# A decoder of two layers on one core: ScalarE copies a step's turned attention weights ahead of the exponentials of a later step

## The chip, the core and the metric

The kernel runs on one core of a Trainium2 chip. Five engines work side by side, each through its own list of instructions in order: TensorE (PE, the matrix products; its weight loads have rows of their own, PEld), VectorE (DVE), ScalarE (ACT), GpSimd (POOL) and SyncE (SP, which starts transfers). They wait for each other through semaphores. The metric is the time of the whole program on the device, in microseconds (us).

## The reference

Two layers, each of attention, cross attention to a short context of 77 rows, and a mixture of experts, on x of 2 x 512 x 128, all in float32. The change lies in the attention of the second layer. Cut to that:

```python
# H, DQ, DV = 16, 64, 64; x is (2, 512, 128)
q = jnp.einsum('bsd,hqd->bhsq', x, w_q)
k = jnp.einsum('bsd,hqd->bhsq', x, w_k)
v = jnp.einsum('bsd,hvd->bhsv', x, w_v)
scores = jnp.einsum('bhsq,bhtq->bhst', q, k)          # causal mask follows
weights = jax.nn.softmax(masked / 8.0, axis=-1)
out = jnp.einsum('bhst,bhtv->bhsv', weights, v)
return jnp.einsum('bsf,df->bsd', cat(out), w_o)
```

Behind it stands a cross attention that keeps the 32 largest of 77 scores for each row and head, and then the experts.

## The kernel before, in words

The order of every engine's work is written out by hand, one block of code for each engine; nothing is scheduled by a planner. The attention of the second layer is a loop of 48 **steps** U = 0 to 47 that every engine's block runs in its own form (`for U in range(NU)`). The 1024 tokens make four blocks of 256. A step takes two heads, and of a block either both tiles of 128 query rows (steps 0 to 7 and 24 to 31, 128 + 256 = 384 columns of weights for a head) or one tile (steps 8 to 23 and 32 to 47, 384 or 512 columns in turn). For one step the work passes from engine to engine:

- TensorE `scores` (L2199) writes the scores to one of two pairs of PSUM banks; it waits until the exponentials of the step two earlier have read that pair.
- VectorE `row_max` (L1131) takes each row's maximum.
- ScalarE `exps` (L1562, instruction L1569) writes the exponentials to SBUF and adds up each row. It is two instructions a head pair or four, each followed by a short one that reads the sum.
- VectorE `row_inv` (L1137) inverts the sums, GpSimd `divide` (L704) multiplies.
- TensorE `turn` (L2228) turns the weights, 128 x 128 at a time, into PSUM banks 4 and 5 and raises `pt_ps`.
- ScalarE `evac_pt` (L1582), called **the copy** below, waits for `pt_ps` and copies the turned weights from those banks to SBUF (`prT`), then raises `ptc_ready`.
- TensorE `values` (L2231) multiplies them with the values of the heads, one step later.

The engines are in different steps at the same time. In the loop's turn U TensorE does the scores of U + 2 and turns the weights of U, ScalarE does the exponentials of U + 2 and the copy of U, GpSimd divides U + 1. Bank 4 has a second user: `project_qk` (L2168) writes a later head pair's queries and keys there, so it waits for the copy of the step before, and the turn behind it waits until ScalarE has copied the queries and keys out (`evac_qk`, L1553).

Around this pair ScalarE's turn has other copies. Ahead of it come the outputs of a head pair (L1577), queries and keys (L1553), values (L1559) and, in some turns, a first half of cross-attention scores (L1609) or of turned cross-attention weights (`weights_T`, L1630). Behind it come, in some turns, the normalised rows (`apply_two`, L1596), a second half of scores (L1609), the other half of turned cross-attention weights (L1630), a copy of a context (L1624), and its exponentials (L1617). TensorE's work for the cross attention shares bank 7, one use after the other: each use waits until ScalarE has copied out the one before.

The two waits that matter here are:

```python
def exps(U):                                  # L1562
    act.wait_ge(nmax_ready, through(U))       # the maximum
    if U >= 3:
        act.wait_ge(pt_ps, U - 2)             # the buffer of step U - 3 has been turned
...
def evac_pt(U):                               # L1579
    act.wait_ge(pt_ps, U + 1)                 # the weights of step U have been turned
```

Of the kernel before, what the change touches and what calls it, by code (L numbers as in the profile page):

```python
# [55 lines left out]
def width(U):  # L56

    c, at, i = UNIT[U][1][-1]
    return at + (c + 1) * P


def piece_of(U):

    if 12 <= U < 28:
        return divmod(U - 12, 4)
    if 29 <= U < 47:
        return 4 + (U - 29) // 3, (U - 29) % 3
    return None, None
# [41 lines left out]
def decoder(nc, x_in, ctx_in, a0_wq, a0_bq, a0_wk, a0_bk, a0_wv, a0_bv, x0_wq, x0_bq, x0_wk, x0_bk, x0_wv,  # L110
# [5 lines left out]
    with ExitStack() as held:  # L116
# [8 lines left out]
        def tiles(bank, width=P):  # L125

            return ps[:, bank, 0:TB * width].rearrange("p (t n) -> p t n", n=width)
# [1289 lines left out]
        def _(act):  # L1417
            def norm_T(n):
                b = NORMS[n][1]
                act.wait_ge(xnT_ps, n + 1)  # L1420
                act.activation(xnT[:, b * S:(b + 1) * S], ps[:, NORM_BANK[n], :], ACT.Copy)\
                   .then_inc(xnT_ready, 1)
# [128 lines left out]
            def evac_qk(j, bank):  # L1551
                act.wait_ge(qk_ps, j + 1)
                act.activation(qk_place(j), ps[:, bank, :].rearrange("p (w n) -> p w n", w=2), ACT.Copy)\  # L1553
                   .then_inc(qk_ready, 1)

            def evac_v(j, bank):
                g, h = j % NP, j // NP % 2
                act.wait_ge(v_ps, j // 2 + 1)
                act.activation(v_all[:, 2 * h:2 * h + 2, g:g + 2, :].rearrange("p t g n -> p t (g n)"),  # L1559
                               ps[:, bank, :].rearrange("p (t n) -> p t n", t=2), ACT.Copy).then_inc(v_ready, 1)  # L1560

            def exps(U):  # L1562
                s = U % 2
                act.wait_ge(nmax_ready, through(U))
                if U >= 3:
                    act.wait_ge(pt_ps, U - 2)
                for c, at, i in UNIT[U][1]:
                    for h in range(2):
                        act.activation(pr[U % 3][:, h, at:at + (c + 1) * P], ps[:, 2 * s + h, at:at + (c + 1) * P],  # L1569
                                       ACT.Exp, bias=nmax[:, i % 8, h:h + 1], accum_out=rsum[:, i % 8, h:h + 1])\  # L1570
                           .then_inc(ex_ready, 1)

            def evac_cat(j):
                act.wait_ge(av_ps, j + 1)
                if j % NP == 0 and j:
                    act.wait_ge(wo_ps, j // NP)
                act.activation(catT[:, j % NP, :], ps[:, 6, 0:2 * P], ACT.Copy).then_inc(cat_ready, 1)  # L1577

            def evac_pt(U):  # L1579
                n = width(U)  # L1580
                act.wait_ge(pt_ps, U + 1)
                act.activation(prT[U % 3][:, :, 0:n], ps[:, 4:6, 0:n], ACT.Copy).then_inc(ptc_ready, 1)  # L1582

            def norm_two(k, done, ready, source):
                act.wait_ge(done, k + 1)
                act.activation(xnT[:, 2 * P * k:2 * P * (k + 1)], source, ACT.Copy).then_inc(ready, 1)

            def evac_qc(k, source):
                act.wait_ge(qc_ps, k + 1)
                act.activation(qc[:, 2 * P * (k % 2):2 * P * (k % 2 + 1)], source, ACT.Identity, bias=bias("x1_bq"))\  # L1590
                   .then_inc(qc_ready, 1)

            def apply_two(k, rstd_done, ready):
                act.wait_ge(rstd_done, k + 1)
                for t in (2 * k, 2 * k + 1):
                    act.activation(xn[:, t, :], x[:, t, :], ACT.Identity, bias=offset[:, t:t + 1], scale=rstd[:, t:t + 1])\  # L1596
                       .then_inc(ready, 1)

            def evac_cn(k, source):
                act.wait_ge(cnT_ps, k + 1)  # L1600
                act.activation(cnT[:, 0:2 * P], source, ACT.Copy).then_inc(cnT_ready, 1)


            def scores(n, t, bank):
                act.wait_ge(half_ps, 2 * n + t + 1)
                if n >= 2:
                    act.wait_ge(gone_ready, n - 1)
                    act.wait_ge(dif_ready, n - 1)
                act.activation(sc[n % 2][:, t, :, :].rearrange("p h n -> p (h n)"), ps[:, bank, 0:4 * NC], ACT.Copy)\  # L1609
                   .then_inc(half_ready, 1)  # L1610

            def weights_x(n):
                q = n % 2
                act.wait_ge(dif_ready, n + 1)
                if n >= 2:
                    act.wait_ge(pkT_ps, 2 * n - 2)
                act.activation(pk[q][:, :, :, :], dif[q][:, :, :, :], ACT.Exp, scale=SCALEX)\  # L1617
                   .then_inc(exc_ready, 1)

            def evac_cx(n, bank):  # L1620
                act.wait_ge(cx_ps, n + 1)
                if n >= 8:
                    act.wait_ge(cn_ready, 2 * (n // 4 - 1))
                act.activation(cx[:, n // 4 % 2, n % 4, :], ps[:, bank, 0:8 * (DX + 1)], ACT.Copy).then_inc(cx_ready, 1)  # L1624

            def weights_T(n, t, bank):
                act.wait_ge(pkT_ps, 2 * n + t + 1)
                if n >= 1:
                    act.wait_ge(cx_ps, n)
                act.activation(pkT[t][:, :, :], tiles(bank)[0:NC], ACT.Copy).then_inc(pkT_ready, 1)  # L1630

            def tokens_high(k):
                act.activation(xt_hi[:, k % 2, :], xnT[:, 2 * P * k:2 * P * (k + 1)], ACT.Copy).then_inc(xin_ready, 1)
# [11 lines left out]
            for U in range(NU):  # L1645
                n, r = piece_of(U)
                spare = ps[:, 7, 0:2 * P]
                for j in range(4 * NP - 1):
                    if U == FIRST[j + 1] + 1:
                        evac_cat(j)  # L1650
                for j in range(3, 4 * NP):
                    if U == FIRST[j] - 3:
                        evac_qk(j, 4)
                        if j in (NP + 2, 2 * NP + 2):
                            tokens_high(j // NP + 1)
                for j in range(2, 4 * NP, 2):
                    if U == FIRST[j] - 1:
                        evac_v(j, 6)
                for k in range(3):
                    if U == STAGE[k + 1] + 3:  # L1660
                        evac_qc(k, spare)
                if U == 12:
                    scores(0, 1, 7)
                if U == 13:
                    scores(1, 1, 7)
                if U == 28:
                    scores(4, 0, 7)
                if r == 0 and n + 1 in EARLY:
                    scores(n + 1, 0, 7)
                if r == 2 and n >= 1:  # L1670
                    weights_T(n - 1, 1, 7)
                if U + 2 < NU:
                    exps(U + 2)
                evac_pt(U)
                for k in range(3):
                    if U == STAGE[k + 1] + 2:
                        apply_two(k, qn_rstd, qn_ready)
                for k in range(2):
                    if U == OUT[k] + 2:
                        apply_two(k, gn_rstd, gn_ready)  # L1680
                if U == 4:
                    norm_T(7)
                if U == 11:
                    scores(0, 0, 7)
                if U == 12:
                    scores(1, 0, 7)
                if U == 28:
                    scores(4, 1, 7)
                if r == 0 and n + 1 in EARLY:
                    scores(n + 1, 1, 7)  # L1690
                if r == 1 and n >= 1:
                    weights_T(n - 1, 0, 7)
                if r == 2 and n >= 1:
                    evac_cx(n - 1, 7)
                if r == 2:
                    weights_x(n)
                for k in range(3):
                    if U == STAGE[k + 1] + 2:
                        norm_two(k, qnT_ps, qnT_ready, spare)
                for k in range(2):  # L1700
                    if U == OUT[k]:
                        evac_cn(k, spare)
                    if U == OUT[k] + 3:
                        norm_two(k, gnT_ps, gnT_ready, ps[:, 6, 0:2 * P])
# [960 lines left out]
```

## Time and profile before

| | us |
|---|---|
| median of 3 runs | 602.57 (597.96 to 604.44) |
| profiled execution, its own time | 589.41 |
| its span, first to last instruction | 587.6 |
| the loop of 48 steps, in the span | about 137 to 392 |

The profile is one execution. Its times are counted from the span's first instruction. A group of rows gives busy time, and the idle time of the engine just before those instructions with what ended it. The loop is 255 us of the 587.6.

### The profile page before, as it was taken

To read this page: it belongs to the slowest core of one execution; us is meant where nothing else is said; L and a number is where in the kernel's file an instruction comes from. 1 tells how busy PE (TensorE), PEld (TensorE's weight loads), DVE (VectorE), ACT (ScalarE), POOL (GpSimd) and SP (SyncE) were. 2 spreads that over 40 slices of the span, in tenths; PEclk is the share of its full clock that TensorE was granted. 3 is DMA by queue.
4 is the path that set the end of the run, shared out by engine and by line. 5 is a ranking of instruction groups with operands and counts; after the bars stand their busy time and mean duration, and the time that the engine had idled before them with its cause. 6 is when DMAs were issued, how large, how long until landed. Compare 5 with 4: busy or idle time off the path is not lost.

```text
span 587.6 us, 12150 instructions
## 1 busy us (share of the span) xinstructions
PE 520.9 (89%) x3954; PEld 413.7 (70%) x3954; DVE 384.4 (65%) x2192; ACT 309.2 (53%) x776; POOL 224.3 (38%) x235
## 2 busy tenths in 40 slices
PE   4888789988898999988999889978999899999997
PEld 2565348846666666767677567667777678999997
DVE  3567865433422598774598899877948979644643
ACT  2343225427875677675875667555775555322222
POOL 5015930013434364662554656552821443430000
PEclk9999999998999999999989999989899999999999
DMA  4600206504000000000000000003510000010000
GB/s 121 204 1 15 63 13 183 171 10 153 1 1 1 1 2 2 1 2 1 2 2 2 2 1 2 1 2 108 176 36 11 15 20 20 19 28 2 28 1 10
DMA packets 24088, 21.03 MB, mean 36 GB/s; under 512 B 2175, under 2 KB 18643, under 8 KB 24027
## 3 DMA queue, kind: packets, MB, share of 16 engines
q1 hardware_dynamic: 23515, 19.21, 10.8%
q0 software_dynamic: 512, 1.05, 0.6%
q8 instruction: 33, 0.54, 0.4%
q14 instruction: 28, 0.23, 0.1%
HBM read 17.22 MB, written 3.03 MB: 34 GB/s over the span
## 4 chain that ended last, share of the span: by engine, by line
PE 65%; DVE 17%; ACT 12%; issue 4%; POOL 1%; DMA 1%; DVEq 0%; ACTq 0%
PE ps L1835 53%; PE ps L2228 4%; DVE nmax L1131 2%; ACT w_mem L1569 2%; ACT prT L1582 2%; PE ps L2290 2%; DVE wk L1186 2%; PE ps L2423 2%; DVE sel_mem L1013 2%; DVE top L1176 2%; ACT f_mem L1534 1%; DVE bn L844 1%; DVE xn L857 1%; PE ps L2482 1%; ACT pr L1569 1%
## 5 line engine op out<-in xcount | busy, mean ns | idle before, releaser
L1131 DVE TENSOR_REDUCE nmax<-ps 128x2 f32<-128x256 f32 (+1 forms) x64 | 51.2, 821 | 66.9 <-PE ps L1835 64.6
L1186 DVE MATCH_REPLACE8 wk<-top,wk 128x77 f32<-128x77 f32 x384 | 80.5, 223 | 0.0
L704 POOL TENSOR_TENSOR w_mem<-w_mem,rinv 128x256 f32<-128x256 f32 (+3 forms) x44 | 53.0, 1216 | 50.8 <-DVE rinv L1137 50.3
L1302 DVE TENSOR_TENSOR sel_mem<-gr,ps 128x512 f32<-128x512 f32 x47 | 32.2, 685 | 50.0 <-ACT gr L1771 49.5
L1771 ACT ACTIVATE gr<-ps 128x512 f32<-128x512 f32 x47 | 28.0, 596 | 60.1 <-PE ps L1835 59.9
L1176 DVE MAX8 top<-wk 128x8 f32<-128x77 f32 x384 | 57.9, 223 | 0.2
L1835 PE MATMUL ps<-cat_mem 64*128 64x256 f32 (+7 forms) x276 | 54.9, 470 | 1.5 <-ACT cat_mem L1553 1.5
L1569 ACT ACTIVATE w_mem<-ps,nmax 128x128 f32<-128x128 f32 (+3 forms) x88 | 44.4, 519 | 12.2 <-DVE nmax L1131 12.2
L735 POOL TENSOR_SCALAR wk<-wk 128x616 f32<-128x616 f32 x16 | 28.0, 1752 | 53.7 <-DVEq L1190 53.4
L1835 PE MATMUL ps<-prT,cat_mem 128*64 128x128 f32 x640 | 43.7, 285 | 1.4 <-DVE x L1211 0.9
L1582 ACT ACTIVATE prT<-ps 128x768 f32<-128x768 f32 (+1 forms) x48 | 42.6, 887 | 0.1
L628 POOL TENSOR_TENSOR rstd<-var_eps,minus_half 128x4 f32<-128x4 f32 x8 | 8.2, 1025 | 88.5 <-DVE var_eps L850 88.4
L1835 PEld LDWEIGHTS ps<-prT,cat_mem 128*64 128x64 f32 x640 | 35.9, 141 | 7.3 <-issue 4.2
L704 POOL TENSOR_TENSOR pr<-pr,rinv 128x768 f32<-128x768 f32 (+3 forms) x20 | 26.6, 1338 | 28.4 <-DVE rinv L1137 28.0
L1553 ACT ACTIVATE cat_mem<-ps 128x512 f32<-128x512 f32 x32 | 19.1, 598 | 32.0 <-PE ps L1835 32.0
L1835 PE MATMUL ps<-fd,sel_mem 128*128 128x128 f32 x256 | 34.5, 278 | 1.5 <-DVE sel_mem L1302 1.5
L2228 PE MATMUL ps<-ident,w_mem 128*128 128x128 f32 x212 | 29.0, 275 | 6.7 <-issue 4.0
L1835 PE MATMUL ps<-later,ident 128*128 128x512 bf16 (+1 forms) x131 | 32.8, 374 | 2.3 <-ACT sc L1609 1.1
L1835 PE MATMUL ps<-x_hi,w_hi 128*128 128x256 f32 x128 | 34.6, 304 | 0.0
L1835 PEld LDWEIGHTS ps<-fd,sel_mem 128*128 128x128 f32 x256 | 31.2, 192 | 2.9 <-DVE sel_mem L1302 2.8
L1835 PE MATMUL ps<-x_hi,w_lo 128*128 128x256 f32 x128 | 31.9, 282 | 0.0
L1835 PEld LDWEIGHTS ps<-vh,sel_mem 77*128 77x128 f32 x256 | 29.9, 192 | 2.4 <-issue 1.2
(352 smaller groups left out, 1338.4 us busy)
## 6 DMA issues: line engine op xcount, KB each, us to landing
w_mem<-in_L_ffn_W_dram SPq DMA_DIRECT2D x12, 256.0 KB, 3.2
f_mem<-in_L_ffn_Wg_dram SPq DMA_DIRECT2D x8, 256.0 KB, 2.8
f_mem<-in_L_ffn_Wu_dram SPq DMA_DIRECT2D x8, 256.0 KB, 3.2
f_mem<-in_L_ffn_Wd_dram SPq DMA_DIRECT2D x8, 256.0 KB, 3.9
sel_mem<-slot_dram SPq DMA_DIRECT2D x7, 256.0 KB
sel_mem<-in_L_ffn_W_dram SPq DMA_DIRECT2D x4, 256.0 KB, 3.9
xs_dram<-zero SPq DMA_DIRECT2D x1, 960.0 KB, 6.0
ys_dram<-f_mem SPq DMA_DIRECT2D x15, 64.0 KB, 1.5
```

Source lines behind the costliest of these rows:

```text
L704: pool.tensor_tensor(pr[s][:, :, at:at + n], pr[s][:, :, at:at + n], rinv[:, i % 8, :].unsqueeze(2).to_broadcast([P, 2, n]), ALU.mult)\
L735: pool.tensor_scalar(wk[q][:, :, :, :], wk[q][:, :, :, :], NEG, None, ALU.is_le)\
L1131: dve.tensor_reduce(nmax[:, i % 8, :], ps[:, 2 * s:2 * s + 2, at:at + (c + 1) * P], X, ALU.max, negate=True).then_inc(nmax_ready, 1)
L1176: dve.max(top[q][:, t, h, 8 * r:8 * r + 8], src[:, t, h, :]).then_inc(top_step, 1)
L1186: dve.match_replace(wk[q][:, t, h, :], top[q][:, t, h, 8 * r:8 * r + 8], src[:, t, h, :], GONE).then_inc(top_step, 1)
L1302: dve.tensor_tensor(hg[s][:, :], gr[s][:, :], ps[:, 2 * s + 1, :], ALU.mult)\
L1553: act.activation(qk_place(j), ps[:, bank, :].rearrange("p (w n) -> p w n", w=2), ACT.Copy)\
L1569: act.activation(pr[U % 3][:, h, at:at + (c + 1) * P], ps[:, 2 * s + h, at:at + (c + 1) * P], ACT.Exp, bias=nmax[:, i % 8, h:h + 1], accum ...
L1582: act.activation(prT[U % 3][:, :, 0:n], ps[:, 4:6, 0:n], ACT.Copy).then_inc(ptc_ready, 1)
L1771: act.activation(gr[j % 2][:, :], ps[:, 2 * (j % 2), :], ACT.Relu).then_inc(gr_ready, 1)
L1835: return pe.matmul(dst, lhsT, rhs, start=start, stop=stop, skip_group_check=shared)
L2228: last = pe.transpose(tiles(4 + h)[:, k, :], pr[U % 3][:, h, k * P:(k + 1) * P], ident[:, :])
```

## The change

Two calls in ScalarE's loop trade places: the copy of step U now stands ahead of the exponentials of step U + 2. Nothing else in the file differs, and the instruction lists of TensorE, VectorE, GpSimd and SyncE are the same as before.

```diff
                 if r == 2 and n >= 1:
                     weights_T(n - 1, 1, 7)
+                evac_pt(U)
                 if U + 2 < NU:
                     exps(U + 2)
-                evac_pt(U)
                 for k in range(3):
                     if U == STAGE[k + 1] + 2:
                         apply_two(k, qn_rstd, qn_ready)
```

ScalarE in turns 10 and 11, before. L1569 are the exponentials, L1582 the copy, L1596 the normalised rows, which wait for GpSimd.

```order
L1569 ACTIVATE w12_mem,rsum<-ps,nmax 128x384 [waits pt_ps,nmax_ready]
L1569 ACTIVATE w12_mem,rsum<-ps,nmax 128x384
L1582 ACTIVATE prT1<-ps 128x2x384 [waits pt_ps]
L1596 ACTIVATE xn<-x,offset,rstd 128x128 [waits qn_rstd]
L1596 ACTIVATE xn<-x,offset,rstd 128x128
L1586 ACTIVATE xnT<-ps 128x256 [waits qnT_ps]
L1577 ACTIVATE sel_mem<-ps 128x256 [waits wo_ps,av_ps]
```

The same place in the changed kernel:

```order
L1582 ACTIVATE prT1<-ps 128x2x384 [waits pt_ps]
L1569 ACTIVATE w12_mem,rsum<-ps,nmax 128x384 [waits pt_ps,nmax_ready]
L1569 ACTIVATE w12_mem,rsum<-ps,nmax 128x384
L1596 ACTIVATE xn<-x,offset,rstd 128x128 [waits qn_rstd]
L1596 ACTIVATE xn<-x,offset,rstd 128x128
L1586 ACTIVATE xnT<-ps 128x256 [waits qnT_ps]
L1577 ACTIVATE sel_mem<-ps 128x256 [waits wo_ps,av_ps]
```

The normalised rows now stand directly behind the exponentials, and the copy ahead of both.

ScalarE in turn 17, before. L1553 copies queries and keys, L1630 copies turned cross-attention weights, the first for this turn and the second for the next.

```order
L1553 ACTIVATE cat_mem<-ps 128x2x256 [waits qk_ps]
L1569 ACTIVATE w12_mem,rsum<-ps,nmax 128x512 [waits pt_ps,nmax_ready]
L1569 ACTIVATE w12_mem,rsum<-ps,nmax 128x512
L1582 ACTIVATE prT2<-ps 128x1024 [waits pt_ps]
L1630 ACTIVATE sel_mem<-ps 77x512 [waits pkT_ps] x2
```

The same place in the changed kernel:

```order
L1553 ACTIVATE cat_mem<-ps 128x2x256 [waits qk_ps]
L1582 ACTIVATE prT2<-ps 128x1024 [waits pt_ps]
L1569 ACTIVATE w12_mem,rsum<-ps,nmax 128x512 [waits pt_ps,nmax_ready]
L1569 ACTIVATE w12_mem,rsum<-ps,nmax 128x512
L1630 ACTIVATE sel_mem<-ps 77x512 [waits pkT_ps] x2
```

The wait for the turned weights (`pt_ps`) now holds back the exponentials and everything behind them.

## Rows read from the trace of the kernel before

**Rows 1.** The page: span; busy time, share and count by engine.

```profile
span 587.6 us, 12150 instructions
PE 520.9 (89%) x3954; PEld 413.7 (70%) x3954; DVE 384.4 (65%) x2192; ACT 309.2 (53%) x776; POOL 224.3 (38%) x235
```

**Rows 2.** Stretches: us, busy by engine (count), granted TensorE clock, DMA share, GB/s.

```profile
137.00:392.00 255.00, 228.91 (x1940) 170.54 (x1939) 180.32 (x1137) 173.31 (x462) 129.82 (x109) 0.99 0.01 4
...
299.50:302.90 3.40, 3.40 (x31) 2.66 (x28) 3.40 (x31) 2.72 (x8) 0.31 (x1) 1.00 0.00 0
302.90:306.30 3.40, 3.40 (x20) 2.48 (x19) 3.17 (x21) 1.70 (x7) 2.25 (x2) 0.50 0.02 5
```

**Rows 3.** Waits of TensorE, 137 to 392: us in total, times, longest us.

```profile
PE ps L1835 <- ACT prT L1582: 2.2, 4, 1.0
PE ps L2264 <- ACT xn L1596: 2.1, 1, 2.1
PE ps L2228 <- ACT prT L1582: 1.9, 5, 0.5
PE ps L1835 <- ACT sel_mem L1630: 1.9, 2, 1.2
PE ps L1835 <- ACT sc L1609: 1.7, 2, 1.1
...
PE ps L2264 <- ACT sel_mem L1624: 0.6, 2, 0.3
```

**Rows 4.** ScalarE by line, 137 to 392: count | busy us, mean ns | idle before.

```profile
L1582 ACT ACTIVATE prT<-ps 128x768 f32<-128x768 f32 x32 | 26.1, 817 | 0.1
...
L1630 ACT ACTIVATE sel_mem<-ps 77x512 f32<-77x512 f32 x18 | 10.6, 590 | 6.7 <-PE ps L2290 6.6
```

**Rows 5.** Timeline, step 23: start us, us, engine, line, operation, [idle before <-releaser].

```profile
252.01 1.06 PE L2228 MATMUL ps<-ident,pr 128*128 128x128 f32 x8
252.11 0.59 ACT L1559 ACTIVATE cat_mem<-ps 128x512 f32<-128x512 f32 x1
...
254.17 1.05 ACT L1582 ACTIVATE prT<-ps 128x1024 f32<-128x1024 f32 x1
...
255.27 0.39 PE L1835 MATMUL ps<-xt_hi,wT_lo 128*128 128x256 f32 x1 [1.02 <-ACT prT L1582]
```

**Rows 6.** Timeline, step 10.

```profile
186.05 0.83 PE L2228 MATMUL ps<-ident,w_mem 128*128 128x128 f32 x6
...
187.82 0.58 ACT L1569 ACTIVATE w_mem<-ps,nmax 128x384 f32<-128x384 f32 x1 [4.85 <-DVE nmax L1131]
...
188.95 0.81 ACT L1582 ACTIVATE prT<-ps 128x768 f32<-128x768 f32 x1
189.64 0.87 ACT L1596 ACTIVATE xn<-x,offset,rstd 128x128 f32<-128x128 f32 x2
```

**Rows 7.** Timeline, step 17.

```profile
220.77 0.60 ACT L1553 ACTIVATE cat_mem<-ps 128x512 f32<-128x512 f32 x1 [1.34 <-PE ps L1835]
...
221.47 1.06 PE L2228 MATMUL ps<-ident,pr 128*128 128x128 f32 x8 [0.73 <-issue]
...
222.61 1.02 ACT L1582 ACTIVATE prT<-ps 128x1024 f32<-128x1024 f32 x1
...
223.51 0.59 ACT L1630 ACTIVATE sel_mem<-ps 77x512 f32<-77x512 f32 x1
...
224.15 0.66 PE L2290 MATMUL ps<-ident,ex_mem 128*77 128x128 f32 x4
```

**Rows 8.** Timeline, step 45.

```profile
381.13 1.04 PE L2228 MATMUL ps<-ident,w_mem 128*128 128x128 f32 x8
...
382.59 0.69 ACT L1569 ACTIVATE pr<-ps,nmax 128x512 f32<-128x512 f32 x1 [1.88 <-DVE nmax L1131]
...
385.48 0.66 PE L2290 MATMUL ps<-ident,ex_mem 128*77 128x128 f32 x4 [2.42 <-ACT sel_mem L1630]
```

**Rows 9.** Timeline, step 39.

```profile
351.35 0.41 PE L2290 MATMUL ps<-ident,ex_mem 128*77 128x128 f32 x2 [0.23 <-POOL ex_mem L742]
```

## The prediction, made before the changed kernel ran

> **What bounds the kernel now.** I read the page first: TensorE is busy 89% of the span and no other engine over 65% [rows 1]. The table of stretches says the same of the loop: TensorE works 228.91 of its 255 us, ScalarE 173.31 [rows 2]. So TensorE sets the pace and the change can pay only out of its 26.1 idle us; ScalarE, which the change reorders, has 81.7 us to spare. The list of waits tells whose products TensorE stands still for. The copy ends 2.2 us of idle in four waits and 1.9 in five; normalised rows end 2.1, turned cross-attention weights (L1630) 1.9 in two waits [rows 3] and 2.42 in another [rows 8], halves of scores 1.7 [rows 3]. In these rows the copy is late because exponentials stand ahead of it on ScalarE, and the others because they stand behind both. The timelines of single turns then show which of the two orders would have served TensorE better.
>
> **What the change does on ScalarE.** Nothing is added or removed: the 48 copies, 0.81 to 1.05 us each [rows 5, 6], and the exponentials stay, and the other engines' lists don't change; no transfer moves. In 46 turns (in the last two there are no exponentials left) the pair trades places. With the copy first it starts when ScalarE is free and the turned weights are there; the exponentials start behind it, or when their maximum is there if that is later. Work behind the pair starts when the pair ends. That gives three kinds of turn.
>
> (a) *The copy itself is waited for.* Step 23: the eight transposes end at 252.01 + 1.06 = 253.07, ScalarE is free at 252.70, yet the copy starts at 254.17, behind exponentials, and TensorE stands still 1.02 us until it ends [rows 5]. With the copy first it runs from 253.1 to 254.2, and TensorE's product can start when the one before it ends, 1.0 us sooner. The next link, the copy of the queries and keys, then finds ScalarE in exponentials: they took from 252.6 to 254.2, so 1.5 us behind the copy's new end, to about 255.6. So 0.3 of the 1.0 is given back. There are nine such waits, 2.2 + 1.9 = 4.1 us [rows 3]. I take off 0.2 for the first, in step 1, where the turn behind it is paced by the queries and keys anyway; 0.3 for step 23; and 0.8 for two of 0.4 around 329 and 348 us, since in that stretch TensorE ends up waiting for GpSimd's product at 351.35 [rows 9], whose chain has neither copy nor exponentials in it. Left: 2.8 us.
>
> (b) *The maximum is late, and something behind the pair is waited for.* Step 10: the transposes end at 186.88, but ScalarE stands idle 4.85 us for the maximum until 187.82, and only then come exponentials, the copy at 188.95 and the normalised rows at 189.64 [rows 6], for which TensorE waits 2.1 us [rows 3]. With the copy first it lies inside that idle time (186.9 to 187.75), and the rows start at 188.9: 0.75 us saved, about one copy. The same holds where ScalarE idles 1.88 us for the maximum in step 45, with TensorE's longest wait of 2.42 us at its end [rows 8]: the transposes end at 381.13 + 1.04 = 382.17, ScalarE gets its maximum at 382.59, so 0.4 of the copy falls into idle time and is saved. A third turn like it is step 44, with a wait of 1.06 us for scores: 0.55. Sum 1.7 us.
>
> (c) *ScalarE is free before the weights are turned.* Step 17: ScalarE is free at 220.77 + 0.60 = 221.37 and today spends the next 1.24 us on exponentials, while TensorE turns the weights until 222.53; the copy starts at 222.61 without loss [rows 7]. With the copy first ScalarE waits out this 1.24 us and does the exponentials later, and the copy gains nothing. What is queued behind it is the turned cross-attention weights at 223.51, and TensorE takes them up at 224.15, at once [rows 7]: they come 1.24 us later, and so does TensorE. Transposes that end after ScalarE is free stand in some 30 of the 46 turns, most of them by 0.3 to 1.2 us, but in most the next item behind the pair is one that ScalarE would idle for, or its taker has time. The ones that bite, worked out in the same way: step 17 with 1.2, step 21 with 0.45, step 25 (0.35 on the existing wait of 1.2 us for L1630 [rows 3]), step 26 (0.3 on one of 0.3 for L1624 [rows 3]). In stage one (steps 0 to 7), losses and gains of 0.15 to 0.25 for the copies of head outputs cancel. Sum 2.3 us.
>
> The later exponentials themselves cost nothing by this reckoning. They move back by at most step 17's wait and copy, 1.24 + 1.02 = 2.3 us [rows 7]. VectorE inverts their sums only behind the next maximum, one turn on, GpSimd's product is taken up another turn later, and the scores that need their bank come two turns on. Going through the turns one by one I find none where the 2.3 us or less reach TensorE that way; if the margin were gone, VectorE would stand waiting for the sums, and GpSimd's product and the transposes would be late next.
>
> **The sum.** 2.8 + 1.7 - 2.3 = 2.2 us off the profiled execution's 589.41, to 587.2. The median of the runs, 602.57, stands 2.2% above that execution; the same share of it gives 600.3 us.
>
> **A bound for the clock.** The granted clock was 2.4 GHz nearly throughout and fell to 1.2 GHz (0.50) for 302.90 to 306.30, where 20 products were done [rows 2]; at the loop's mean of 1940 in 255 us it would have been 25.9, so one such stretch costs 5.9 products, 0.8 us, and at most half of its 3.4 us. TensorE was busy through the 3.4 us before it fell [rows 2], so I can't say that the change adds or removes such a stretch, and keep 0.8 either way for the range.
>
> **The rivals.**
>
> *Only gains.* The losses (c) are local arithmetic. If ScalarE's spare 81.7 us swallow them, 4.5 us are won: 598.0. For it: nearly every wait in (c) is followed by idle time of ScalarE. Against it: in step 17 the taker starts 0.05 us after its weights are copied, so nothing is there to swallow it. Chance 0.22.
>
> *Nothing.* What TensorE wins at the copy it loses at its next wait for ScalarE, as at step 23 with a third of it; the clock, or VectorE and GpSimd in the last third of the loop, take the rest. 602.6. Chance 0.21.
>
> *Slower: the wait for the turned weights holds up ScalarE's queue.* This is (c) at every place where turned cross-attention weights stand directly behind the pair. ScalarE has 18 copies of them, two for each of nine pieces [rows 4], and one of each two stands there; if all nine slip by step 17's 1.24 us and are taken up at once, 11.2 us are lost against 4.5 won: 6.7 us slower, 609.4. It decides where the transposes end more than about 1 us after ScalarE is free and TensorE's next use of bank 7 follows within that. For it: steps 17 and 21 are so. Against it: in the others I found the transposes done sooner or the taker later. Chance 0.12.
>
> The Trainium skill speaks for this rival: "TensorE: Matmul & The Clock Gate", section "Architectural detail: the array is 16× 32×32, not 1× 128×128", says that ScalarE's queue is a strict FIFO, so that nothing can pass a copy that waits. By that rule taken alone, with no slack anywhere, the time would be the rival's 609.4. The trace agrees on the order: in step 10 the copy, ready at 186.88, stood behind exponentials until 188.95 [rows 6]; what it doesn't decide is whether anyone waits for what is held up.
>
> **How the numbers follow.** The forecast has 0.45. The likeliest time is 600.3. The range must take in 598.0 and 602.6 and the clock's 0.8 on either side, scaled, and the spread of the runs shown (597.96 to 604.44, so 4.6 below and 1.9 above the median): about half of that spread below the first gives 595.5, and it all above the second with the clock gives 606. The slow rival lies outside. A difference under 1%, here 596.5 to 608.6, can't be told from none in this kernel. Faster than that needs the only-gains case with luck, 0.14; slower needs the slow rival, 0.09; the rest is 0.77.
>
> **What would show it.** In the profile after, the row of TensorE's waits for the copy should fall from 4.1 us to about 1; step 10's wait for normalised rows from 2.1 to about 1.3; the copy of step 10 should lie inside the wait for the maximum. ScalarE should show new idle time ended by TensorE in front of the copy (L1582), near zero now [rows 4], of 10 us or more, and TensorE a new wait of over 1 us for L1630 in step 17. TensorE's idle time in the loop should fall from 26.1 to about 24. I am wrong if the new waits for L1630 or for the queries and keys exceed what the copy's waits give back, or if VectorE's maxima come later because scores do.

## The result: about 3 us gained at equal clock, hidden under a spread of 14

Timed beside the kernel before on the same chips, the changed kernel took 590.17 us (median of 19 runs, 586.72 to 597.2) against 595.7 (19 runs, 590.8 to 604.44): a ratio of 0.9932, interval 0.9903 to 0.996. (Ratios, here and below, leave out runs over 1.5% above the fastest of their kernel; medians do not.) Timed again on another chip the ratio was 0.9996, interval 0.9952 to 1.004. The forecast had the sign and a change of under 1%, but the measured 590.17 lies outside 595.5 to 606, and even the kernel before was not where the forecast had put it: 595.7 and not 602.57. The granted clocks of the 19 runs before are not on record, so this pair alone can't tell how much of the 5.5 us between the medians is the order.

**The profile after.** The page's span and busy times, which answer to [rows 1]:

```profile
span 588.2 us, 12150 instructions
PE 522.5 (89%) x3954; PEld 416.3 (71%) x3954; DVE 384.5 (65%) x2192; ACT 311.6 (53%) x776; POOL 224.5 (38%) x235
```

The span is 0.6 us longer than before, 590.0 us as a run. The table of stretches says why (columns as in [rows 2]: us, busy by engine, granted clock); the first row is the loop, the other two a stretch at half clock and the one ahead of it:

```profile
137.40:392.40 255.00, 230.07 (x1941) 173.22 (x1939) 181.16 (x1142) 175.41 (x462) 130.29 (x110) 0.98 0.01 4
272.68:276.09 3.41, 2.71 (x25) 2.30 (x25) 1.12 (x11) 3.41 (x14) 0.00 (x0) 1.00 0.00 0
276.09:279.50 3.41, 3.41 (x17) 2.85 (x14) 2.44 (x15) 0.70 (x2) 1.27 (x2) 0.50 0.00 0
```

TensorE's idle time in the loop fell from 26.1 to 24.9 us, but its busy time rose by 1.2 for the same work: the granted clock was at half for 3.41 us three times (from 276.09, 320.47 and 385.32), before only once [rows 2].

TensorE's waits in the loop (us in total, times, longest), against [rows 3]:

```profile
PE ps L2290 <- ACT sel_mem L1630: 4.6, 4, 2.0
PE ps L1835 <- ACT sel_mem L1630: 2.3, 2, 1.6
PE ps L2264 <- ACT xn L1596: 1.4, 1, 1.4
PE ps L1835 <- ACT sc L1609: 1.2, 2, 0.7
PE ps L2264 <- ACT sel_mem L1624: 1.0, 2, 0.7
```

Both rows of waits for the copy, 4.1 us, are gone; the waits for normalised rows and scores shrank, those for L1630 and L1624 grew. ScalarE's side, by line (count | busy us, mean ns | idle before), against [rows 4]:

```profile
L1582 ACT ACTIVATE prT<-ps 128x768 f32<-128x768 f32 x32 | 26.1, 814 | 10.6 <-PE ps L2228 10.0
L1582 ACT ACTIVATE prT<-ps 128x1024 f32<-128x1024 f32 x16 | 16.4, 1024 | 11.2 <-PE ps L2228 11.2
```

ScalarE now idles 21.2 us in front of the copy, for the transposes: the "10 us or more" of the prediction.

The turns themselves. The timeline (start us, us, engine, line, operation, [idle before <-releaser]) of step 23, as [rows 5]:

```profile
251.05 1.06 PE L2228 MATMUL ps<-ident,pr 128*128 128x128 f32 x8
...
252.15 1.02 ACT L1582 ACTIVATE prT<-ps 128x1024 f32<-128x1024 f32 x1 [0.41 <-PE ps L2228]
...
253.23 0.39 PE L1835 MATMUL ps<-xt_hi,wT_lo 128*128 128x256 f32 x1
...
254.65 0.62 ACT L1553 ACTIVATE cat_mem<-ps 128x512 f32<-128x512 f32 x1
255.37 0.85 PE L2228 MATMUL ps<-ident,w_mem 128*128 128x128 f32 x6 [1.17 <-issue]
```

TensorE no longer waits 1.02 us for the copy, and as predicted finds the copy of the queries and keys (L1553) late: its wait there is 1.17 us, from 0.73 before. Step 10, as [rows 6]:

```profile
185.46 0.83 PE L2228 MATMUL ps<-ident,w_mem 128*128 128x128 f32 x6
186.32 0.81 ACT L1582 ACTIVATE prT<-ps 128x768 f32<-128x768 f32 x1 [2.94 <-PE ps L2228]
187.23 0.58 ACT L1569 ACTIVATE w_mem<-ps,nmax 128x384 f32<-128x384 f32 x1
...
188.36 0.87 ACT L1596 ACTIVATE xn<-x,offset,rstd 128x128 f32<-128x128 f32 x2
189.37 0.41 PE L2264 MATMUL ps<-ident,xn 128*128 128x128 f32 x2 [1.41 <-ACT xn L1596]
```

The copy lies inside the wait for the maximum and the rows come 1.41 us after TensorE is free, not 2.1. Step 17, as [rows 7]:

```profile
219.32 1.06 PE L2228 MATMUL ps<-ident,pr 128*128 128x128 f32 x8 [0.73 <-issue]
...
220.42 1.02 ACT L1582 ACTIVATE prT<-ps 128x1024 f32<-128x1024 f32 x1 [1.20 <-PE ps L2228]
...
222.66 0.59 ACT L1630 ACTIVATE sel_mem<-ps 77x512 f32<-77x512 f32 x1
223.31 0.66 PE L2290 MATMUL ps<-ident,ex_mem 128*77 128x128 f32 x4 [1.43 <-ACT sel_mem L1630]
```

The predicted loss: the copy waits 1.20 us, the exponentials go behind it, and TensorE stands 1.43 us for L1630, which was taken up at once before. Step 45's wait [rows 8] went from 2.42 to 2.04 us:

```profile
384.37 0.66 PE L2290 MATMUL ps<-ident,ex_mem 128*77 128x128 f32 x4 [2.04 <-ACT sel_mem L1630]
```

and around step 39 TensorE's wait for GpSimd's product grew from 0.23 [rows 9] to 0.45 us, where what steps 35 and 38 had won is given back:

```profile
351.17 0.63 PE L2290 MATMUL ps<-ident,ex_mem 128*77 128x128 f32 x4 [0.45 <-POOL ex_mem L742]
```

### The profile page after: what moved, and what is told of

Read it like the earlier page. It is cut to its first block, busy times and chain, and to the rows that moved or that the text cites. A ratio compares the mean times of both kernels' runs of the same rounds, so it can differ in the third digit from the quotient of the medians.

```text
span 588.2 us, 12150 instructions
## 1 busy us (share of the span) xinstructions
PE 522.5 (89%) x3954; PEld 416.3 (71%) x3954; DVE 384.5 (65%) x2192; ACT 311.6 (53%) x776; POOL 224.5 (38%) x235
## 4 chain that ended last, share of the span: by engine, by line
PE 66%; DVE 16%; ACT 9%; issue 5%; POOL 2%; DMA 1%; DVEq 0%; ACTq 0%; POOLq 0%
PE ps L1835 54%; PE ps L2228 5%; ACT w_mem L1569 2%; DVE wk L1186 2%; PE ps L2290 2%; PE ps L2423 2%; DVE sel_mem L1013 2%; ACT f_mem L1534 1%; DVE top L1176 1%; DVE nmax L1131 1%; DVE bn L844 1%; DVE xn L857 1%; PE ps L2482 1%; PE ps L1847 1%; DVE sel_mem L1302 1%
## 5 line engine op out<-in xcount | busy, mean ns | idle before, releaser
L704 POOL TENSOR_TENSOR w_mem<-w_mem,rinv 128x256 f32<-128x256 f32 (+3 forms) x44 | 53.1, 1218 | 48.5 <-DVE rinv L1137 47.9
L1582 ACT ACTIVATE prT<-ps 128x768 f32<-128x768 f32 (+1 forms) x48 | 42.4, 884 | 21.8 <-PE ps L2228 21.3
L1569 ACT ACTIVATE w_mem<-ps,nmax 128x128 f32<-128x128 f32 (+3 forms) x88 | 44.5, 522 | 1.8 <-DVE nmax L1131 1.7
L704 POOL TENSOR_TENSOR pr<-pr,rinv 128x768 f32<-128x768 f32 (+3 forms) x20 | 26.6, 1340 | 30.1 <-DVE rinv L1137 29.8
L1553 ACT ACTIVATE cat_mem<-ps 128x512 f32<-128x512 f32 x32 | 19.2, 600 | 25.0 <-PE ps L1835 24.8
```

The costliest lines, as they stand in the source:

```text
L704: pool.tensor_tensor(pr[s][:, :, at:at + n], pr[s][:, :, at:at + n], rinv[:, i % 8, :].unsqueeze(2).to_broadcast([P, 2, n]), ALU.mult)\
```

## A measure that the clock leaves alone

Where no stretch at half clock intervenes, the loop repeats to a few hundredths of a us from run to run. So the kernels can be compared by when TensorE starts the transposes of a step, counted from those of step 0. After: step 17 at 219.32, step 0 at 143.56, so 75.76; before 221.47 [rows 7] and 143.13, so 78.34; the change is 2.58 us ahead there. All kernels so, in us against the first profile of before (the last four are experiments):

| first transposes of step | before again | after | after again | gains_only | losses_only | late_max | best_again |
|---|---|---|---|---|---|---|---|
| 8 | -0.01 | -0.92 | -0.91 | -0.90 | -0.01 | 0.03 | -0.92 |
| 11 | 0.01 | -1.72 | -1.70 | -1.60 | -0.01 | -0.66 | -2.72 |
| 17 | 0.01 | -2.58 | -2.56 | -2.48 | -0.01 | -0.65 | -4.11 |
| 18 | 0.01 | -1.28 | -1.26 | -2.48 | 1.30 | -0.65 | -4.12 |
| 22 | 0.00 | -1.39 | -1.38 | -2.98 | 1.67 | -0.65 | -4.64 |
| 26 | 0.00 | -1.65 | -1.63 | -3.64 | 3.64* | -0.64 | -5.80 |
| 46 | 1.52* | -1.54* | -1.47* | -4.00* | 5.06* | -1.23* | -7.15* |

A star: stretches at half clock lie between. One costs up to 1.6 us: before again jumps from -0.03 to 1.53 between steps 34 and 35, over its stretch from 329.42, gains_only from -3.64 to -2.07 between 26 and 27, over its from 280.07. (The stretch of before at 302.88 cost 1.23: late_max, which has none there, gains that between steps 31 and 33.)

## The experiments

The first four ran on one chip. Theory S: the time follows TensorE's idle time in the loop. Theory C: what the timed runs show beyond that is the clock.

**control**: the kernel before, unedited.

> The kernel before itself, unchanged, timed against itself, to see the granted clock of each of its runs. Theory S (the order alone: the time follows TensorE's idle time in the loop) expects a ratio of 1.000 and a mean granted clock near the 0.984 of its profiled execution, no lower than that of the changed kernel (0.978 in the middle of its 19 runs). Theory C (the clock: the 4 us that the change brought in the timed runs, against 1.3 us less idle time in the profiled ones, are half-clock stretches that the old order has more often) expects 1.000 too, but a middle clock of its runs below 0.978, 0.970 or so: the runs of the changed kernel lie on a line of 4.7 us for each 0.01 of the clock, so 0.008 would be the 4 us.

Measured 592.91 us (12 runs, 589.41 to 596.38), ratio 0.9996, interval 0.9953 to 1.0038. The same instructions ran at clocks from 0.974 (596.37 us) to 0.986 (590.87). Over 134 runs of nine kernels (those that the ratios use, with their clocks, and the four single profiled ones) a line with one slope and a level for each kernel gives 4.9 us for each 0.01 of clock, and scatters by 1.2 us about it. "At equal clock" below means the distance between two such levels, with its standard error. Where the longer runs lose shows in control's stretches ahead of the loop:

```profile
36.00:49.50 13.50, 9.53 (x57) 6.69 (x56) 8.99 (x38) 6.13 (x13) 1.01 (x1) 1.00 0.00 0
49.50:59.70 10.20, 10.20 (x36) 6.00 (x34) 5.44 (x24) 1.40 (x5) 7.33 (x10) 0.50 0.08 22
```

Behind a stretch in which TensorE had 4 us of idle time in gaps of under 1 us, its clock was at 1.2 GHz for 10.2 us; in the first profile of before it stayed at 2.4 GHz there, behind gaps much like these (3.3 us in the same 13.5). So the gaps alone don't decide it. The copy of step 0 came at 151.15 us, not 144.46. The change doesn't touch that part of the program. The middle clock, 0.977, was neither S's 0.984 nor C's 0.970: the one profiled execution is one draw from a wide spread.

**after_again**: the changed kernel, unedited.

> The changed kernel again, beside the control on one chip. Theory S expects 0.993 to 0.997 (1.3 to 4 us) at the same clock as the control. Theory C expects 0.993 with a clock 0.005 or more above the control's, and a difference of 2 us or less between runs of the two that have the same clock.

593.81 us (12 runs), ratio 0.9996, interval 0.9952 to 1.004. S's range is missed, and so is C's sign: its clock was not higher than the control's but lower, with a middle of 0.972 against 0.977. Yet copy by copy its loop is that of the first trace of the change to 0.2 us, and at equal clock it is 2.5 us ahead on this chip (standard error 0.5), 2.9 over the 134 runs (0.3), and 2.6 over all 152 with a clock on record. So C fell in the form that the old order draws more half clock. What stands is that the clock of a set of runs differs by chance by as much as the change is worth.

**gains_only**: old order except in 14 turns.

```diff
+                first = U in (0, 1, 3, 5, 10, 13, 15, 19, 23, 27, 35, 38, 44, 45)
+                if first:
+                    evac_pt(U)
                 if U + 2 < NU:
                     exps(U + 2)
+                if not first:
+                    evac_pt(U)
```

> The pair trades places only in 14 turns (0, 1, 3, 5, 10, 13, 15, 19, 23, 27, 35, 38, 44, 45), where the profile before has TensorE waiting for the copy or for work behind a late maximum; the other turns keep the old order. Theory S expects the gains without the losses, 4.5 us less than before by the sum of the prediction: 0.992, and 2.3 to 2.8 us less than the changed kernel; TensorE's waits for the copy near 0 and its wait for L1630 in step 17 absent. The rival that the losses are swallowed elsewhere expects the time of the changed kernel. Theory C expects a time that follows the clock and not the 2.5 us.

590.55 us (12 runs), ratio 0.9963, interval 0.9925 to 1.0002; at equal clock 4.7 us under before (error 0.4), the forecast's 4.5, and 1.8 under the changed kernel, where 2.3 to 2.8 were expected. In step 17 nothing is lost; timeline:

```profile
228.31 0.59 ACT L1630 ACTIVATE sel_mem<-ps 77x512 f32<-77x512 f32 x1
228.95 0.66 PE L2294 MATMUL ps<-ident,ex_mem 128*77 128x128 f32 x4
```

TensorE (its line numbers are 4 higher here) takes L1630 up without a wait. The losses are not swallowed elsewhere: the table has gains_only 1.2 us ahead of the change at step 18, and 2.0 at 26. (Its waits for the copy are not all gone: one of 0.52 us stands ahead of the transposes of step 42, for a copy left in the old order.)

**losses_only**: the same edit with `U in (17, 21, 25, 26)`.

> The pair trades places only in turns 17, 21, 25 and 26, where ScalarE is free before the weights are turned. Theory S expects 2.3 to 2.8 us more than before: 1.004 to 1.005, with the new waits of TensorE for L1630 of 1.4 us in step 17 and 0.6 in step 21, and 0.4 more in 25 and for L1624 in 26. The rival that later slack swallows them expects 1.000.

600.39 us (6 runs), ratio 1.0127, interval 1.0055 to 1.0198. Over half of that is clock (0.962 to 0.983); at equal clock it is 2.7 us over before (error 0.6). Its waits, against [rows 3]:

```profile
PE ps L2294 <- ACT sel_mem L1630: 4.8, 4, 2.4
PE ps L1839 <- ACT sel_mem L1630: 2.3, 2, 1.6
PE ps L2268 <- ACT sel_mem L1624: 1.0, 2, 0.7
```

The waits for L1630 are 7.1 us; before they were 1.9 [rows 3], 2.42 [rows 8] and a 0.4, 4.7 in all: 2.4 more, with 0.4 for L1624. In the table the loss is 1.30 at step 17, and 0.39 at 21 (1.28 to 1.67). Gains_only plus losses_only give the change: -2.48 + 1.30 = -1.18 against -1.28 at step 18.

**late_max**: the same edit with `U in (10, 44, 45)`; one profiled run.

> The pair trades places in turns 10, 44 and 45 alone, the three where the maximum is late. By the sum of the prediction 0.75 + 0.55 + 0.4 = 1.7 us less, each in its own place: TensorE's wait for normalised rows in step 10 1.4 us for 2.1, for the second half of scores in step 44 0.5 for 1.06, for L1630 in step 45 2.0 for 2.42, and the copies of all steps between unchanged but for a shift of 0.7. The rival that the gain of step 10 is given back before the next of them expects the copy of step 17 at the same distance from that of step 0 as before, 78.3 us.

598.67 us at a clock of 0.969, which says nothing; its trace does. 0.66 us ahead from step 11 on, kept to the end (-0.64 at 26); then -0.31 at step 44, -0.85 at 45, -1.23 at 46: 0.66 + 0.54 + 0.38 = 1.58 us for the predicted 1.7. The rival, that step 10's gain is given back, falls.

**turned_first**: the changed kernel with the first L1630 of a turn ahead of the exponentials; one profiled run.

```diff
                 evac_pt(U)
+                if r == 1 and n >= 1:
+                    weights_T(n - 1, 0, 7)
                 if U + 2 < NU:
                     exps(U + 2)
...
-                if r == 1 and n >= 1:
-                    weights_T(n - 1, 0, 7)
```

> The changed kernel, with the first copy of turned cross-attention weights (L1630) moved ahead of the exponentials in every turn that has one, so that only the exponentials are late. It tests two steps of the prediction: that the losses are the late L1630 and nothing else, and that later exponentials cost nothing. If so, TensorE's new waits for L1630 (1.4 us in step 17, 0.6 in 21, 0.4 in 25) go or halve, the wait of 2.0 in step 45 falls to about 0.7, and the loop is 2 to 3 us shorter than the changed kernel's at the same clock. The rival, that the exponentials have no room, expects new waits of TensorE for GpSimd's product (L704) of 0.5 us or more each in the turns behind 17, 21, 25 and 45, and no gain.

595.35 us at a clock of 0.964, 5.3 us under before at that clock by a single run (error 1.3). Step 17's loss is gone (-2.59 at step 18, for -1.28). But nothing is won in step 21 (-1.36 at step 22, for -1.39). Timeline:

```profile
246.86 0.58 ACT L1630 ACTIVATE sel_mem<-ps 77x512 f32<-77x512 f32 x1
247.34 0.68 ACT L1569 ACTIVATE pr<-ps,nmax 128x512 f32<-128x512 f32 x1
248.00 0.68 ACT L1569 ACTIVATE pr<-ps,nmax 128x512 f32<-128x512 f32 x1
248.67 0.60 ACT L1553 ACTIVATE cat_mem<-ps 128x512 f32<-128x512 f32 x1
...
249.36 0.84 PE L2228 MATMUL ps<-ident,w_mem 128*128 128x128 f32 x6 [0.69 <-issue]
```

TensorE waits 0.69 us for the copy of the queries and keys instead of for L1630. The later exponentials are not the cause. That copy starts 3.83 us behind the first transposes of step 21 here, and 3.82 us in the changed kernel, where the same works stand ahead of it in another order (3.43 in the kernel before). It is late in both because ScalarE first stood idle 1.20 us for the turned weights. And the 2.0 us wait of step 45 fell to 0.71, but behind it TensorE waits again:

```profile
384.89 1.04 PE L2228 MATMUL ps<-ident,w_mem 128*128 128x128 f32 x8
...
389.07 0.41 DVE L1211 TENSOR_TENSOR x<-x,ps 128x256 f32<-128x256 f32 x1
...
389.53 1.75 PE L1835 MATMUL ps<-prT,cat_mem 128*64 128x128 f32 x28 [0.67 <-DVE x L1211]
...
391.65 1.89 POOL L704 TENSOR_TENSOR pr<-pr,rinv 128x1024 f32<-128x1024 f32 x1
...
393.59 1.63 PE L2228 MATMUL ps<-ident,pr 128*128 128x128 f32 x8 [0.43 <-POOL pr L704]
```

In the kernel before, without those waits:

```profile
385.32 0.40 DVE L1211 TENSOR_TENSOR x<-x,ps 128x256 f32<-128x256 f32 x1
...
387.89 1.89 POOL L704 TENSOR_TENSOR pr<-pr,rinv 128x1024 f32<-128x1024 f32 x1
```

Its transposes of step 47 are 1.34 us less ahead than those of step 46. Here too it is not the exponentials, which are 1.0 us later than before. Counted from the first transposes of step 45 (384.89 here, 381.13 before [rows 8]), VectorE's context sum (L1211) starts after 4.18 us here and 4.19 before, and GpSimd's product (L704) after 6.76 us in both. TensorE comes sooner and meets the pace of these two engines. So the L1630s are the loss, as expected; putting them first pays in steps 17 and 25 (-2.53 at step 26, for -1.65), in part in 45 and not in 21. The rival's waits of 0.5 us or more for GpSimd's product did not come.

**best**: gains_only, with what TensorE waits for put ahead in four turns.

```diff
                 if first:
                     evac_pt(U)
+                if U == 10:
+                    apply_two(0, qn_rstd, qn_ready)
+                if U == 45:
+                    weights_T(n - 1, 0, 7)
                 if U + 2 < NU:
                     exps(U + 2)
+                if U == 11:
+                    scores(0, 0, 7)
+                if U == 25:
+                    weights_T(n - 1, 0, 7)
                 if not first:
                     evac_pt(U)
```

(The same calls are taken out of their old places.)

> The pair trades places in the 14 turns of gains_only, and in four turns what TensorE waits for goes ahead: the normalised rows of step 10 and the turned weights L1630 of step 45 between the copy and the exponentials, the scores of step 11 and the L1630 of step 25 between the exponentials and the copy. From the trace of gains_only: the rows could start when their scale is there, 1.1 us sooner; L1630 of step 45 1.3 sooner; the scores of step 11 0.9 (of a wait of 0.65); L1630 of step 25 0.5. Theory S expects 2.5 to 3.5 us less than gains_only and 7 to 8 less than before at the same clock, a ratio of 0.987 to 0.990 if the clocks come out alike. The rival, that exponentials 0.6 to 0.9 us later hold up GpSimd's product and the transposes, expects the time of gains_only, 4.5 us less than before at the same clock.

583.78 us (6 runs), ratio 0.9858, interval 0.9808 to 0.9908. Its waits: step 10's for normalised rows is 0.3 (2.1 before), step 45's for L1630 0.7:

```profile
PE ps L1845 <- DVE x L1211: 2.1, 2, 1.5
PE ps L2300 <- ACT sel_mem L1630: 0.7, 1, 0.7
PE ps L2274 <- ACT xn L1596: 0.3, 1, 0.3
```

(Its line numbers are 10 higher.) VectorE's context sum (L1211) now heads the waits for another engine, with 2.1 us for 0.9 in the first profile of before. Timed again:

> The kernel of best again, since its six runs had a mean clock of 0.9835, higher than the 0.9775 of the unchanged kernel's, and 0.006 of clock is 2.8 us by the line of 4.7 us for each 0.01. Theory S with theory C expects the same 7 us less at the same clock, and a ratio between 0.985 and 0.990, nearer to 0.988 if the clocks come out alike. The rival that the first ratio of 0.986 was the order alone expects 0.986 at whatever clock.

585.86 us (6 runs), ratio 0.9882, interval 0.9807 to 0.9956, at a middle clock of 0.982. Over both sets it is 6.9 us under before at equal clock (error 0.4), just short of the 7 to 8 expected. By order alone it was 9.0 ahead at step 46 (-7.15, less two stretches of 1.5 and 1.6, plus the 1.23 of before), and 1.34 of that went at step 47, as in turned_first (-7.15 to -5.81, no fall of the clock between). The sum and the product start 4.18 and 6.77 us behind step 45's first transposes here too, so it is again VectorE's and GpSimd's pace that TensorE meets at the loop's end. The rival, that the later exponentials eat up the gain, falls.

**busier**: the old order, with more filler products (outputs read by nobody) ahead of the loop. The expectation speaks of 34; the edit adds 31, and the trace has 3985 products for 3954.

```diff
+            keep_busy(7, 3)
             weights_T0(1)
+            keep_busy(7, 3)
             context0(1)
             keep_busy(7, 3)
...
-            keep_busy(7, 8)
+            keep_busy(7, 10)
...
-                    keep_busy(6, 4)
+                    keep_busy(6, 6)
```

> The order of the kernel before, with 34 more filler products (128x512 in bf16, about 0.22 us each at full clock, outputs read by nobody) on TensorE in the idle times of the routing stage ahead of the loop, 36 to 80 us, where the unchanged kernel's slower runs have TensorE at half clock for 6.8 to 10.2 us from 49 us on and again at 84 us. Theory C (the spread of the runs and the basis of 602.57 are granted clock, and the clock falls there after TensorE has stood idle for 0.3 to 0.7 us at a time) expects the falls at 49 and 84 us gone, the copy of step 0 at about 144.5 us in the trace and not at 150 to 151, a middle clock of 0.983 or more against the control's 0.977, and a ratio of 0.990 to 0.995. The rival, that the clock falls there whatever TensorE does, expects the same spread and a ratio of 1.000 to 1.005 (the fillers at half clock take longer than the idle time).

592.32 us (12 runs), ratio 1.0006, interval 0.9965 to 1.0047: no gain, clocks from 0.967 to 0.986 with a middle of 0.980, not the 0.983 expected. Its second trace:

> A second trace of busier. If the fillers take the falls at 49 and 84 us away whatever the run, this trace has none there either, and the copy of step 0 starts before 146.5 us. The rival, that the first trace was luck (the unchanged kernel has runs without them too), expects a fall there in about one of two traces, and the copy of step 0 at 149 to 152 us.

593.36 us. In both traces the falls between 48 and 91 us are gone, and the copy of step 0 starts at 146.03 and 145.11 us; of the eleven traces without the fillers nine have falls there. The first one's stretches, the same two as of control and the loop:

```profile
36.00:49.50 13.50, 11.53 (x66) 7.49 (x67) 9.00 (x38) 5.94 (x13) 1.01 (x1) 1.00 0.00 0
49.50:59.70 10.20, 10.06 (x63) 6.40 (x63) 6.81 (x30) 4.48 (x10) 7.92 (x11) 1.00 0.08 22
...
143.00:390.00 247.00, 224.29 (x1852) 166.97 (x1850) 170.65 (x1071) 163.97 (x438) 124.06 (x104) 0.97 0.01 1
```

But the loop had 0.97 of the clock (0.98 in the second trace), against 0.99 in the first profile of before and in control. So the falls can be filled away where they were, and the time does not follow. That the clock falls elsewhere instead, because of the fillers, is not shown: control_look below has seven falls in its loop without them. Half of what was expected came, and not the half that counts.

**best_busy**: best and busier together.

> The kernel of best with the 34 fillers of busier ahead of the loop. If the falls of the clock at 49 and 84 us are what makes slow runs, and the fillers take them away (busier's trace shows none there, with the copy of step 0 at 146.0 us and not at 150), the runs lie closer together than those of best, none below a clock of 0.975, with a median 1 to 3 us under best's. The rival from busier's own runs (clock 0.967 to 0.986, ratio 1.0006): the clock falls elsewhere instead, and the time is that of best.

581.14 us, ratio 0.9809, interval 0.9753 to 0.9865: the best kernel, and the steadiest. All six runs lie at 0.990 or 0.991, 580.5 to 582.26 us. At equal clock it is no better than best (6.3 under before, error 0.6), so what it adds is clock. The loop's row:

```profile
143.00:390.00 247.00, 227.41 (x1948) 171.82 (x1949) 177.94 (x1135) 170.04 (x446) 130.94 (x108) 0.99 0.01 2
```

Why the fillers steady the clock with this order and not with the old one isn't settled; six runs on one chip may be luck in part.

**control_look**: the kernel before, a third trace.

> A third trace of the kernel before. The loop up to its first half-clock stretch is expected to be the same to 0.05 us as in the other two, copy by copy; a stretch at half clock there costs 1.0 to 1.6 us. Whether it has the falls ahead of the loop decides the copy of step 0: 144.5 us without, 149 to 152 with.

605.54 us at 0.955, with half clock from 48.33 to 58.57 and for 24 us in the loop; the copy of step 0 came at 152.06. Up to the first stretch in the loop every copy lies within 0.03 us of the first profile's; that stretch cost 1.58 us.

## Why the prediction was wrong, step by step

**The step that failed is "the same share of it gives 600.3 us".** It took the 2.2% between the profiled execution and the median of three runs for a property of the kernel that the changed one would share. It was the spread of three runs: the sixteen runs that joined them have a middle of 594.6, later medians of the same kernel were 595.7, 594.78, 592.85 and 595.68, and single runs lay between 587.26 and 605.54 at clocks from 0.994 to 0.954. Three runs between 597.96 and 604.44 were the upper part of that spread. Their own clocks are not on record; by the line, 602.57 would be a clock of about 0.957 for the profiled run's 0.984. That it was their clock is therefore inferred, not shown. The range, cut from those three, could not reach the 590.17 that came. On the line of the clock the profiled 589.41 itself was the better basis for a clock like its own.

**The bound for the clock** was too low twice. A stretch at half clock in TensorE-bound work costs 1.0 to 1.6 us in these traces, not 0.8, and so up to nearly the "at most half of its 3.4 us". And their number differs: the three traces of before have 4, 10 and 24 us at half clock between the copies of steps 0 and 47, and 3, 17 and 20 us ahead of them. One stretch more or less was allowed for, not ten.

**Gains (a), 2.8 us, mis-sized**: about 4.0. gains_only at step 46 is -4.00 with one stretch of 1.57 more than before, so -5.6 by order alone; less the 1.6 of late_max, 4.0 are left. The rows of waits understate a stall on TensorE. In step 0 before, the product that waits for the copy shows 0.19 of idle time:

```profile
144.77 0.39 PE L1835 MATMUL ps<-later_t,ident 128*128 128x256 bf16 x2
...
145.35 0.38 PE L1835 MATMUL ps<-xt_hi,wT_lo 128*128 128x256 f32 x1 [0.19 <-ACT prT L1582]
```

and after, without the wait:

```profile
145.20 0.39 PE L1835 MATMUL ps<-later_t,ident 128*128 128x256 bf16 x2
145.34 0.36 PE L1835 MATMUL ps<-xt_hi,wT_lo 128*128 128x256 f32 x1
```

From start to start it is 0.58 us before and 0.14 after: the stall was 0.44. Back to back the starts are closer than the recorded durations, and idle time is counted from an end. The Trainium skill, "Perfetto Trace Analysis", section "Tensor Engine Instruction (MATMUL, LD_WEIGHTS)", says that a product's reported end is estimated from its size and not observed; the 0.19 against 0.44 agrees. Step 1's product, 149.50 to 150.04 before, shows no idle time in the view and lost about as much. Not every stall was won, though. Step 0's 0.44 went at once to GpSimd's product for step 1, which comes at the same distance from step 0 in both kernels; after:

```profile
147.45 0.85 PE L2228 MATMUL ps<-ident,w_mem 128*128 128x128 f32 x6 [0.44 <-POOL pr L704]
```

What stayed came from steps 1, 3 and 5 (0.45, 0.41 and 0.52 in gains_only, of which 0.47 was lost again by step 7). So the first eight steps gave 0.92 us, where I had the gains and losses of stage one cancel but for 0.3. That is about half of what the sum lacked. The rest came behind it: 0.31, 0.31 and 0.61 us of idle time for the copies of steps 15, 19 and 27 were worth 0.47, 0.48 and 0.88.

**Gains (b), 1.7 us, right**: 0.66, 0.54 and 0.38 for 0.75, 0.55 and 0.4.

**Losses (c), 2.3 us, right**: 1.30 in step 17 for 1.2, 0.39 in 21 for 0.45, 0.38 in 25 for 0.35, 0.38 in 26 for 0.3 (by its wait for L1624): 2.45. Steps 35 and 38 gave back what they won, as taken off.

**Later exponentials cost nothing**: right where the traces were read for it. Gains_only and losses_only add up to the change within 0.1 us as far as step 26, and where turned_first won nothing (step 21) or gave a gain up again (step 47, as best did), the exponentials were not the cause. In step 21 of turned_first they did put off VectorE's inversion (L1137) and GpSimd's product by 0.3 us, and TensorE didn't wait for it.

**The sum** of 2.2 us was 2.9 at equal clock (error 0.3), and 3.4 by order alone at step 46: -1.54, less its stretches of 1.57 and 1.56, plus the 1.23 that one cost before. (a), (b) and (c) as measured make 3.1; the other 0.3 lies behind step 26, and no run places it.

**The rivals.** *Only gains* falls by losses_only. *Nothing* is what after_again's ratio of 0.9996 looks like, and its traces show that the gain was there under a lower clock. *The slower rival* named a real mechanism in the wrong number: new waits for L1630 in steps 17 and 21 and a longer one in 25, 2.4 us in all for its 11.2. By the rule of the Trainium skill that went with it ("TensorE: Matmul & The Clock Gate", section "Architectural detail: the array is 16× 32×32, not 1× 128×128") ScalarE's queue lets nothing pass a waiting copy; step 17 agrees, with 1.20 us of idle time ahead of the copy and L1630 behind it.

## What to carry to other kernels

Before a forecast is scaled to a median, ask what separates the profiled run from it: if it is the granted clock, compare kernels at equal clock, or by starts within the trace where no stretch at half clock lies between. When two works of one queue trade places, decide turn by turn (which of the two is late, and who waits for what is behind) and keep the old order where the moved one isn't ready; here that turned 2.9 us into 4.7, and moving the works behind them too into 6.9. Size a stall on TensorE from start to start, and ask whose pace it meets next: step 0's 0.44 us and 1.34 us of best's gain ended at GpSimd and VectorE.

## What was not expected of the hardware

The clock fell to 1.2 GHz in stretches of 3.41 to 13.65 us: between 48 and 91 us behind work with no idle gap of 1 us, and twelve times in the loops of these traces right behind 3.4 us in which TensorE was busy throughout (first at 302.88 of the first profile [rows 2], also at 308.94 of control, and at 239.48 and 386.25 of control_look). Which stretches are hit differs from run to run of the same program, and it is most of the spread: 0.994 at 587.26 us, 0.955 at 605.54. Not every one costs time: losses_only lost 1.58 us over its stretch from 349.71 and had it back one step later, where TensorE otherwise waits 0.92 us for VectorE and 0.41 for the copy.
